# Signalling each quad's spread queries by a DRAIN in a graph attention kernel

## What is computed

```python
for r in range(5):                                   # edge types
    mask = edge_types == r
    q = einsum('eh,khd->ekd', x[dst], W_Q[r])        # query of each edge's destination
    k = einsum('eh,khd->ekd', x[src], W_K[r])
    v = einsum('eh,khd->ekd', x[src], W_V[r])
    logits = (q * k).sum(-1) / 4 + attn_bias[r]
    attn = softmax of logits over the edges of this type with the same dst
    out = out + segment_sum(attn * v, dst)
h = out @ out_proj_w.T + out_proj_b + x
x = layernorm(x + layernorm(h) * gamma + beta)
```

## Time and profile before

| | |
|---|---|
| median of three runs | 1296.82 us |
| the profiled execution, its span | 1301.8 us |
| TensorE (PE) matmuls busy | 938.5 us, 72% |
| weight loads (PEld) busy | 827.1 us, 64% |
| DVE busy | 1002.1 us, 77% |
| ACT busy | 547.3 us, 42% |
| POOL busy | 763.0 us, 59% |
| chain that ended last | DVE 36%, issue 28%, unknown queue 16%, PE 14% |
| granted TensorE clock from the third slice on | 0.5 of full speed |
| POOL's 784 gathers (L1699) | 745.6 us busy, 951 ns each |
| products of the spread queries (L1807), 2352 | 293.5 us busy, 309 ns each, overlapping |

### The profile page before, as it was taken

The page is one execution under the profiler, slowest core; times in us unless marked ns, Lnnn a source line. Parts: engine busy times, 40 slices in busy tenths (PEclk is TensorE's granted clock), DMA queues, the critical chain, the costliest instruction groups (busy, mean ns, idle before and its releaser), DMA issues.

```text
span 1301.8 us, 19088 instructions
## 1 busy us (share of the span) xinstructions
PE 938.5 (72%) x5180; PEld 827.1 (64%) x5180; DVE 1002.1 (77%) x1851; ACT 547.3 (42%) x1044; POOL 763.0 (59%) x859
## 2 busy tenths in 40 slices
PE   9924467866778767877787776877677677666777
PEld 4513456765667656766676765767576666666677
DVE  3656678877878778878878788887788788778996
ACT  5624443444434444444444444444444334343322
POOL 0067666666666666666666666666666666666640
PEclk9956555555555555555555555555555555555555
DMA  8976555554655555555654555655555455555410
GB/s 318 379 216 180 168 159 172 157 160 144 166 159 156 148 157 167 157 139 166 174 161 145 146 164 157 182 140 152 162 168 148 136 140 155 146 141 154 131 48 12
DMA packets 121376, 209.26 MB, mean 161 GB/s; under 512 B 22845, under 2 KB 79546, under 8 KB 121166
## 3 DMA queue, kind: packets, MB, share of 16 engines
q0 software_dynamic: 37632, 102.81, 27.8%
q1 hardware_dynamic: 79602, 92.61, 23.8%
q10 hardware_dynamic: 4032, 12.57, 2.5%
HBM read 176.92 MB, written 30.99 MB: 160 GB/s over the span
## 4 chain that ended last, share of the span: by engine, by line
DVE 36%; issue 28%; another core or an unknown queue 16%; PE 14%; ACT 2%; DVEq 2%; DMA 1%; ACTq 0%; POOL 0%; POOLq 0%; SPq 0%
DVE LT L1324 6%; DVE pool L1416 4%; PE pp L1863 4%; DVE av L666 4%; DVE pool L1387 4%; DVE pool L1288 3%; PE pp L572 3%; DVE pool L1310 2%; PE pp L1807 2%; DVE Tt L1300 2%; DVE Yt L1373 2%; DVE ohn L650 2%; PE pp L1846 2%; DVE Mt L1402 2%
## 5 line engine op out<-in xcount | busy, mean ns | idle before, releaser
L1699 POOL DMA_INDIRECT ring<-KVtab,kvi x784 | 745.6, 951 | 491.0 <-issue 207.3
L1807 PE MATMUL pp<-qwin,pool 128*128 128x128 bf16 x2352 | 293.5, 309 | 73.5 <-issue 53.4
L1863 PE MATMUL pp<-ohn,av 128*128 128x32 f32 x1464 | 328.1, 392 | 20.6 <-issue 18.5
L1863 PEld LDWEIGHTS pp<-ohn,av 128*128 128x128 f32 x1464 | 324.4, 328 | 22.1 <-issue 18.7
L1807 PEld LDWEIGHTS pp<-qwin,pool 128*128 128x128 bf16 x2352 | 262.9, 151 | 112.9 <-issue 111.4
L1310 DVE TENSOR_TENSOR pool<-pp,ring 128x512 f32<-128x512 f32 x196 | 133.5, 681 | 81.9 <-remote 67.3
L909 ACT ACTIVATE Et<-pool 120x512 f32<-120x512 f32 (+1 forms) x66 | 41.6, 630 | 293.2 <-DVE pool L1288 160.5
L1884 PE MATMUL pp<-pool,negb 128*128 128x512 bf16 (+1 forms) x84 | 37.3, 444 | 169.2 <-ACT pool L897 107.4
L882 ACT ACTIVATE pool<-rkb,npid 128x512 bf16<-128x512 bf16 x196 | 139.4, 711 | 36.2 <-DMA rkb<-Ktab 18.9
L1846 PEld LDWEIGHTS pp<-sel,pool 120*128 120x128 f32 (+1 forms) x536 | 129.5, 326 | 38.5 <-issue 38.4
L666 DVE TENSOR_TENSOR av<-ring,pp 128x512 f32<-128x512 f32 x183 | 124.2, 679 | 34.2 <-remote 34.0
(11 more groups left out here) (133 smaller groups left out, 969.1 us busy)
## 6 DMA issues: line engine op xcount, KB each, us to landing
rkb<-Ktab SPq DMA_DIRECT2D x196, 128.0 KB
mk<-Mtab SPq DMA_DIRECT2D x201, 100.2 KB
qwin<-Qfast SPq DMA_DIRECT2D x196, 96.0 KB
KVtab<-pool SPq DMA_DIRECT2D x25, 640.0 KB, 6.3
ring<-KVtab,kvi POOLq DMA_INDIRECT x784
Qfast<-pool ACTq DMA_DIRECT2D x21, 480.0 KB
Qfast<-ring SPq DMA_DIRECT2D x4, 480.0 KB
xs<-in_x_b SPq DMA_DIRECT2D x5, 320.0 KB
```

Source lines behind the costliest of these rows:

```text
L1699: e.indirect_dma_start(kv[:, home(m), j, :], None, KV, bass.IndirectOffsetOnAxis(kvi[:, 4 * q + j:4 * q + j + 1], 0)).then_inc(kv_in[m % 6 ...
L1807: last = e.matmul(pp[2 + m % 2][:, j * C:(j + 1) * C], ohr[:, m % OR, j * C:(j + 1) * C], qwin[:, m % 3, k * C:(k + 1) * C], start=(k == 0 ...
L1863: last = e.matmul(sums_at(f)[:, 0:n], weighed_at(f)[:, j, :], hot_at(f)[:, j, 0:n], start=(j == 0), stop=(j == 3))
```

## The change

TensorE's last product of a quad no longer increments `q_expanded`. Behind the twelve products stands a DRAIN on TensorE, and the DRAIN increments it. There are 196 quads, so 196 DRAINs. Nothing else is changed: the waits, the other signals and the order of all other instructions stay.

```diff
@@ -1806,7 +1806,7 @@
                     for k in range(3):
                         last = e.matmul(pp[2 + m % 2][:, j * C:(j + 1) * C], ohr[:, m % OR, j * C:(j + 1) * C],
                                         qwin[:, m % 3, k * C:(k + 1) * C], start=(k == 0), stop=(k == 2))
-                last.then_inc(q_expanded, 1)
+                e.drain().then_inc(q_expanded, 1)
 
             def turn(i, n):
```

## The result

The changed kernel takes 1308.81 us (median of 4 runs, 1306.74 to 1313.16), beside 1296.49 us for the kernel before (4 runs, 1294.86 to 1297.39): 1.0102 times as long, 95% interval 1.0081 to 1.0122, or 12 us more. The direction is the one forecast; the size is a third of the 38 us.

The account below looks back on a forecast made before the run. The prediction took TensorE's completions, held while POOL gathers back to back, to set the pace. Profiled 1301.8 us plus 38 us for the heavy steps gave 1340, or 1335 us on the median; range 1255 to 1420 us.

Parts of the forecast that it names:

- What bounds the kernel: Quad stretch: no engine is full; TensorE's completions are held during back-to-back gathers and POOL pauses for them, 5.98 us a quad.
- Step (1): DRAIN's signal when nothing holds it: 0.04 us a quad later, at most 8 us in all.
- Step (2): TensorE work queued behind the DRAIN: 0.35 us a quad, 67 us of TensorE's time, hidden where there is a pause.
- Step (3): DRAIN among gathers: held as the products' completion is, each hold that of four gathers, floor staying 6.0 us a quad.
- Step (4): TensorE's work between DRAINs: steps of 6.58, 5.82 and 4.72 us; only the two-collect step exceeds 6.0, plus 38 us.
- the floor of 6.0: POOL's gathers: about 6 us a quad, as the next run starts 5.99 us after a run of four began.
- The test written for this step: New profile, TensorE's DRAINs: if they are long and the pace is 5.98 us all the same, step (4) was wrong.
- the other signs: New profile: L1310 still released "remote"; DRAIN rows microseconds long among gathers, near 0.4 us past 1240 us.
- Step (5): DVE gets turned logits 2.0 us later once in three quads, hidden by idle time; uncovered, it would add 128 us.
- A: Rival: the DRAIN's signal escapes the hold and POOL's runs grow; faster, 1237 to 1285, about 1265 us; chance 0.30.
- B: Rival: each DRAIN waits out a pause as long as after eight gathers; 1543 us, or 1420 with half; chance 0.12.
- C: Rival: no change; DRAIN held, floor stays, light steps make up the heavy one; 1294 to 1299 us; chance 0.13.

Follow-up runs that it names:

- set 3: Third set, kernel before at 1297.79 us: without gathers from the nineteenth quad 1116.93 us, with plain transfers by SP 1096.69, by POOL 1092.49.
- e0_after: The changed kernel itself, run again beside the kernel before in a set where signals weren't held: 1110.50 us against 1109.12, ratio 1.0006.
- e1_both: Kernel before with a DRAIN without increment behind the last product, which keeps its own increment: 1296.39 us, ratio 1.0104.
- Set 1: First set, kernel before at 1281.95 us: DRAIN only ahead of steps with two collects 1294.24 us, only at the other two thirds 1291.40.
- e4_two: Kernel before with two DRAINs in a row behind the products, the second carrying the increment: 1305.85 us, ratio 1.0174.
- e12_near_rows: Kernel before gathering rows near one another, by the sorted destinations, in a set where signals weren't held: 1109.08 us, ratio 1.0002.

## Why the prediction was right in direction and wrong in size

**What bounds the kernel** was read right. The pauses end with TensorE's late signals, and TensorE's completions are late while gathers are made: in set 3 taking the gathers away, or making them plain transfers, brought every signal of the quads without gathers back to 0.33 to 0.35 us, and 175 to 205 us with it. Not foreseen was that this isn't constant from set to set.

**Step (1), the signal's time in quiet**, 0.04 us: measured 0.007 (0.335 against 0.328). Nothing hangs on it.

**Step (2), the queue behind**, 0.35 us a quad: 0.44 measured in the tail, and hidden as forecast where nothing is held (1.8 us with no gathers, 1.4 in e0_after). The restart in it was put at 0.1 us with no row behind it; in the tail it and the signal are 0.23 together. Under the hold TensorE's waits only moved, to the collects (100.2 us in place of 18.5) and away from other lines: its whole idle time in the stretch is 330 us after 328.

**Step (3), the hold**: "the DRAIN is held as the products' completion is" is right. A DRAIN ends 1.8 us behind the last product's start in the median, against 0.33 in quiet, a second one behind it takes 13 ns, and e1_both costs what the change costs, though its increment is still the product's. "Each hold is that of a run of four" holds for most: 117 runs of four with 1.3 us pauses, 29 of eight left.

**Step (4) is the one that failed**, in its words "only the first exceeds 6.0, by 0.6", times 64. It sized the heavy step at 6.58 us, and 6.75 was measured; but it let the other two stand at the floor of 6.0, and they take 5.80 and 5.58. The floor was a mean, not a bound for each step. The heavy step loses 0.75 and the light ones give back 0.20 and 0.42: 0.13 is left for three quads by these means, 8 us in 64 turns (5.4 us by the pace, 0.029 us times 187 quads). The timeline at 665.9 shows how it is given back, and the last column how often: a light step's DRAIN is over before POOL has made its fourth gather, 24 times of 59 behind turn and back, and the next four gathers start without a pause. Set 1 measures the term alone: the 65 DRAINs ahead of heavy steps cost 12.3 us, not 38. The others, priced at nothing, cost 9.5 alone, but only 2.1 on top of the heavy ones. That the light DRAINs cost so much alone isn't explained by the giving back.

Even the 6.58 was right by luck, by two errors that cancel. I had added busy times that overlap: up to the last product's start the heavy step takes 5.23 us, with the quiet 0.33 that makes 5.56, not 5.98 plus 0.35, and the 0.25 from the signal to the gather lies outside TensorE's cycle. By work alone it would stay under 6.0. And I had let it have no hold, but it still has one: 1.52 us from the last product to the DRAIN's end, though POOL's gathers are mostly over by then (the DRAIN ends 1.56 us after the last gather does, in the median; 1.01 and 0.99 for the other two). The test written for this step said so: DRAINs long, and the pace all but the same. Two of the other signs were badly chosen. L1310 isn't released "remote" any more but by the DRAIN's name, and the DRAIN records past 1240 us are 2.2 to 3.9 us long and not 0.4, since a record begins ahead of the products.

**Step (5), DVE's cover.** L1387's idle time went from 31.1 to 84.4 us in the page's groups, 53 us, so DVE does get the turned logits later; forecast was 2.0 us, 64 times, 128 us, hidden. Most of it was hidden: the total cost is 12 us, and DVE's whole idle time in 97 to 1240 us is 242 us after 239.

**The rivals.** A (the signal escapes) fell: POOL's waits rose to 229.7 us, and e1_both shows that the carrier makes no difference. The Trainium skill's rule behind it ("Perfetto Trace Analysis", sequencer-only instructions), that the sequencer itself pushes a DRAIN's update, may be right, but it decides nothing: the update comes when the DRAIN is over, and the DRAIN is held. The Trainium skill's rule that a drain waits until the engine is fully idle ("PSUM — Partial Sum Buffer", engine and sequencer instructions) agrees with the trace: the second of two DRAINs takes 13 ns. B (slower by far) fell: the pauses after the 117 runs of four are 1.3 us, not 2.3. C, "the heavy step is made up by the light ones", was the mechanism, though not to the full: two thirds of the 38 us are given back, and 12 remain that a measurement tells from none. The forecast and C weren't exclusive; a number between the two would have been the better one.

**What stays open.** Why some sets are held and others free wasn't found: program, gathers (950 ns in both) and bytes are the same, and so is the time that the gathers' packets took (27.8% of 1301.8 us in before, 32.5% of 1109.2 in e0_after, both about 361 us). What in a gather delays TensorE's completions isn't shown either, nor whether the scattered rows or the indirect form are needed for it. Whether POOL's wait for q_expanded or the queue behind the DRAIN carries the remaining 12 us wasn't settled, since both sets made for it were free; that TensorE stops is what e1_both shows to cost, but by which of the two it reaches the pace isn't told. No version that still computes the layer was faster than the kernel before: those that are faster leave gathers out or load other rows.

## What to carry to other kernels

When steps of unequal weight share a floor, price the whole cycle, not its heaviest step: ask whether the floor holds for each step or only for their mean, because the light ones give back what the heavy one loses. A DRAIN used as a signal costs what it keeps from running behind it, and next to nothing for the signal itself; where its engine's completions were late, it stood for 1.8 us each time, of which a few hundredths of a microsecond a quad came through to the end. And before a small effect is explained, look whether the kernel before takes the same time in every set: here the condition, at 13 to 15%, was an order larger than the change, and in one of its two states the change costs nothing.

## What the runs showed of the hardware that was not expected

- TensorE's completions (signals of products and ends of DRAINs alike) can be late by microseconds while POOL makes indirect gathers: in the kernel before about 3.4 us in the median and up to 12.5 us between the last product's start and its signal, against 0.33 us without gathers, with plain transfers, or in the free sets. DVE's signals to ACT aren't late in the same trace (0.03 us). The whole kernel takes 1282 to 1298 us in the one condition and 1109 to 1111 in the other, 13 to 15% less.
- In the held condition replacing the gathers by plain transfers that POOL issues itself gives 1092 us: issuing as such isn't what holds. Whether it is the indirect form, the scattered rows or POOL's longer work isn't shown. A plain one takes POOL 538 ns, an indirect one 951.
- A DRAIN behind a DRAIN takes 13 ns and ends 79 ns after it (e4_two); under the hold 196 of them still cost 9.5 us.
- The held traces record far fewer semaphore updates: 6652 in before, 26821 in e0_after.
- TensorE, stopped by a DRAIN and with nothing held, loses 0.44 us to the start of its next products: they start 0.55 us behind the last product's start in e0_after, 0.11 in e12_near_rows.
